# Five pairs of 16-bit products of 512 columns taken out of the second attention

## The chip, the cores and the metric

The kernel runs on one core of a Trainium2 chip. The metric is the device time of one execution in microseconds (us). Three executions of the kernel before took 310.08, 311.3 and 319.42 us, median 311.3. TensorE is written PE below, VectorE DVE, ScalarE ACT, GpSimd POOL.

## The reference

The input x has four sequences (b = 0 to 3) of 256 tokens with 256 channels, in 32-bit floats. Four layers follow each other, and each of them starts with the same gating step:

```
x = x + attn0(cond(x))        # 16 heads of 16 columns, softmax over rows and over columns
x = x + ffn0(cond2(x))        # 8-bit product of 256 by 256, and a bias
x = x + attn1(cond(x))        # rotary, block mask, softmax, 16 heads
x = x + ffn1(cond2(x))        # BitLinear: h = relu(xq w1)^2 (1024 wide), then hq w2
```

cond is a running weighted sum over time, forward and backward, that is divided and multiplied by a sigmoid of x. In ffn1 the weights are rounded to -1, 0 and 1 and the activations are scaled by the largest value of each row, so each row has to be known before it can be quantised.

The kernel writes only the final x. The products that the change takes out have a result that nothing reads: they belong to no term of the reference.

## The kernel before, in words

Each engine has a program of its own, and the programs meet by semaphores. The order of the work is written out by hand, in slots. In the second attention and the last layer a slot is one value of `p` in `for p in SLOTS1`, from -8 to 41; the programs of PE, ACT, DVE and POOL all run over the same `p`. Slots 0 to 31 are the 32 pairs of heads (8 for each sequence). Tables such as `HID_AT`, `TURN_AT`, `DOWN_AT`, `X_AT` say in which slot a piece of the last layer for tile t (128 rows) or sequence b is done, so the last layer of a sequence runs beside the attention of the next ones.

PE does, in this order in each slot: the scores of the slot (`scores1`, L1436), the turning of an attention output (`turn_y1`, L1475), the approximate scores from which a row maximum is taken for a slot four later (`maxima`, L1415), the transposes of queries (`turn_again`, L1467), probabilities by values (`values1`, L1451), the turning of finished rows (`turn_rows`, L1208), projections of the next sequence, then the pair of products of the change, and last the last layer: `turn_hidden` (L1538), `turn_x` (L1514), `hidden` (L1529), `down` (L1552). The scores wait for ACT's exponential of the slot before (L661); `maxima` waits for DVE's row maximum (L981) and for DVE's `relu` (L1034) where both use the same bank; `hidden` waits for DVE's row maxima; `turn_x` waits for DVE's quantised rows (L1015); `down` waits for copies by ACT (L589) or DVE (L1020), and its result is added by DVE at L1063.

The helper `whole(bank, n)` issues n products of a 128x128 16-bit identity with 512 columns of a 16-bit weight tile, into a bank of PSUM; nobody reads the result. It is called in several places: before and in the first feed-forward layer, in slots -4 to -1, twice in each of the slots 23 to 27, and three times in each of the slots 36, 38, 40 and 41. In slots 23 to 27 it stands behind a wait for `g3_done` at 2, which ACT reaches in slot 20, and it writes bank 0 of `PM`, which no other instruction uses in those slots.

POOL starts the DMAs that add the backward to the forward sums, and SP those that load and store; neither runs in step with these products.

Of the kernel before, what the change touches and what calls it, by code (L numbers as in the profile page):

```python
# [71 lines left out]
def build(nc, xT_d, kT_d, vec_d, cond_d, gains_d, gcol_d, attn0_d, attn0p_d, ffn0_d, bias0_d, attn1_d, w1_d, w2_d,  # L72
          ident_d, rope_d, out_d):
    ctx = ExitStack()
    with ctx:
# [3 lines left out]
        S = {n: ctx.enter_context(nc.semaphore(n)) for n in LOADS + STEPS}  # L79
# [107 lines left out]
        PM = ctx.enter_context(nc.psum_tensor("PM", [P, 2, 512], F32))  # L187
# [68 lines left out]
        def tiles(table, p):  # L256
            return [t for t, at in enumerate(table) if at == p]

        def again_at(p):
            q, odd = divmod(p + 2, 2)  # L260
            return [] if odd or not 0 <= q < B * CH else [divmod(q, CH)]

        def turny_at(p):
            return tiles(TURNY_AT, p)
# [856 lines left out]
        def _(pe):  # L1121
# [83 lines left out]
            def turn_rows(q, bank, ready, done):  # L1205
                pe.wait_ge(S[ready], q + 1)
                for u in range(TT):
                    ins = nc.tensor.transpose(PO[:, bank, T + u * P:T + (u + 1) * P], yc[:, q % 2, u * P:(u + 1) * P],  # L1208
                                              ident[:])
                ins.then_inc(S[done], 1)  # L1210
# [111 lines left out]
            def whole(bank, n):  # L1322
                for i in range(n):
                    nc.tensor.matmul(bank, identb[:], w1q[:, 0:512], start=True, stop=True)
# [66 lines left out]
            def maxima(n):  # L1391

                b, j = divmod(n, PAIRS)
                c = j // 2
                if j == 0:
                    pe.wait_ge(S["kTb_done"], b + 1)
                    pe.wait_ge(S["qTb_done"], b + 1)
                if n == 0:
                    pe.wait_ge(S["y8_done"], B)
                    pe.wait_ge(S["v1_done"], 1)  # L1400
                elif n == 1:
                    pe.wait_ge(S["kT1_done"], 1)
                elif n == 2:
                    pe.wait_ge(S["negmax_done"], 2)
                else:
                    pe.wait_ge(S["negmax_done"], 2 * n)
                rounded = [t for t, at in enumerate(HID_AT) if at < n - LEAD]
                if rounded:
                    pe.wait_ge(S["relu_done"], len(rounded))
                at0 = max_bank(n)  # L1410
                q, k = qTb[b % 2], kTb[b % 2]
                for u in range(TT):
                    for i in range(2):
                        r = SLOT * (2 * (j % 2) + i)
                        ins = nc.tensor.matmul(PS[:, at0 + i, u * P:(2 * u + 1) * P],  # L1415
                                               q[r:r + ROWS, c, u * P:(u + 1) * P],
                                               k[r:r + ROWS, c, 0:(u + 1) * P], start=True, stop=True)
                ins.then_inc(S["mx_mm_done"], 1)

            def scores1(p):  # L1420

                b, j = divmod(p, PAIRS)
                c = j // 2
                if j % 2 == 0:
                    pe.wait_ge(S["po1_free"], PO1["again", b, c] + 1)
                if j == 0:
                    pe.wait_ge(S["kT1_done"], b + 1)
                if p == 0:
                    pe.wait_ge(S["negmax_done"], 4)
                q, k = qT1[b % 2], kT1[b % 3]  # L1430
                for v in range(TT):
                    for i in range(2):
                        if v == 0 and p >= 1:
                            pe.wait_ge(S["e1_done"], 2 * (p - 1) + i + 1)
                        r = SLOT * (2 * (j % 2) + i)
                        ins = nc.tensor.matmul(PS[:, i, 2 * v * P:2 * P + v * P], k[r:r + ROWS, c, v * P:(v + 1) * P],  # L1436
                                               q[r:r + ROWS, c, v * P:2 * P], start=True, stop=True)
                        if v == TT - 1:
                            ins.then_inc(S["s1_done"], 1)

            def values1(q):
                b, c = divmod(q, CH)
                pe.wait_ge(S["e1_done"], 4 * q + 4)
                if c == 0:
                    pe.wait_ge(S["v1_done"], b + 1)
                    pe.wait_ge(S["v_ones"], 1)
                if q >= 1:
                    pe.wait_ge(S["y1_done"], q)
                for v, q0, col in ((0, 0, 0), (1, P, 2 * P)):
                    for g in range(4):  # L1450
                        ins = nc.tensor.matmul(PO[SLOT * g:SLOT * (g + 1), 0, q0:T], vt[:, b % 3, v * H + 4 * c + g, :],  # L1451
                                               E[:, (2 * q + g // 2) % 4, g % 2, col:col + T - q0],
                                               start=(v == 0), stop=(v == TT - 1))
                ins.then_inc(S["pv1_done"], 1)
# [7 lines left out]
            def turn_again(b, c):  # L1462
                pe.wait_ge(S["negmax_done"], 2 * (PAIRS * b + 2 * c + 2))
                free1(("again", b, c), downs(PAIRS * b + 2 * c - 2))
                for u in range(TT):
                    src = kp[:, b % 2, u * H + 4 * c:u * H + 4 * c + 4, :]
                    ins = nc.tensor.transpose(PO[:, 1, u * P:(u + 1) * P], src.rearrange("p g s -> p (g s)"), ident[:])  # L1467
                ins.then_inc(S["qre_done"], 1)

            def turn_y1(b):  # L1470
                pe.wait_ge(S["y1_done"], CH * (b + 1))
                free1(("rows", b), downs(TURNY_AT[b]))
                for h in range(HALF):
                    for u in range(TT):
                        ins = nc.tensor.transpose(PO[:, 1, h * T + u * P:h * T + (u + 1) * P],  # L1475
                                                  ytok[:, u, h * P:(h + 1) * P], ident[:])
                ins.then_inc(S["ytr1_done"], 1)
# [78 lines left out]
            for p in SLOTS1:  # L1556
                b, j = p // PAIRS, p % PAIRS
                if -LEAD <= p < 0:
                    whole(PO[:, 0], 3)
                if 0 <= p < B * PAIRS:  # L1560
                    scores1(p)
                for bb in turny_at(p):
                    turn_y1(bb)
                if 0 <= p + LEAD < B * PAIRS:
                    maxima(p + LEAD)
                for bb, c in again_at(p):
                    turn_again(bb, c)
                if p % 2 == 0 and 0 <= (p - 2) // 2 < B * CH:
                    values1((p - 2) // 2)
                if p % 2 == 1 and 0 <= (p - 3) // 2 < B * CH:  # L1570
                    turn_rows((p - 3) // 2, 0, "rows1_done", "turned1_done")
                for t in tiles(QK_AT, p):
                    project_qk(t // TT, t % TT)
                if j == 1 and b + 1 < B:
                    project_v(b + 1)
                if p == -PAIRS + 2:
                    turn_both()
                if j == 2 and 0 < b + 1 < B:
                    turn(b + 1, 0, "qtr_done", [("qkp_done", 2 * TT * (b + 2)), ("v1_done", b + 2),
                                                ("rope_done", TT * (b + 2)), ("v_ones", 1)])  # L1580
                if j == 3 and 0 < b + 1 < B:
                    turn(b + 1, TT * H, "ktr_done", [("qTb_done", b + 2)])
                for bb in tiles(G3_AT, p):
                    turn_gates(bb)
                for bb in tiles(STATE_AT, p):
                    state_rows(bb)
                for bb in tiles(PROJ_AT, p):
                    project_rows(bb)
                if p in (23, 24, 25, 26, 27):
                    pe.wait_ge(S["g3_done"], 2)  # L1590
                    whole(PM[:, 0], 2)
                if p in (36, 38, 40, 41):
                    pe.wait_ge(S["g3_done"], B)
                    whole(PM[:, 0], 3)
                for t in tiles(TURN_AT, p):
                    turn_hidden(t)
                for bb in tiles(X_AT, p):
                    turn_x(bb)
                for t in tiles(HID_AT, p):
                    hidden(t)  # L1600
                for t in tiles(DOWN_AT, p):
                    down(t)
# [59 lines left out]
```

## Time and profile before

| | |
|---|---|
| median of three executions | 311.3 us (310.08 to 319.42) |
| profiled execution, its own time | 313.35 us |
| its span, from first to last instruction | 311.5 us |
| PE busy | 266.2 us (85%) |
| DVE busy | 254.0 us (82%) |
| ACT busy | 204.7 us (66%) |
| POOL busy | 37.1 us (12%) |
| mean granted TensorE clock | 0.949 of full speed |
| chain that ended last | PE 46%, DVE 27%, ACT 13%, issue 9%, DMA 3% |

The profiled execution is one execution: 1.85 us of its time lie outside the span. Busy PE counts a product from its issue to the modelled end of its pipeline, so a product of 0.38 us may block its follower for less. The granted clock is 1.00 at 2.4 GHz and 0.50 at 1.2 GHz. In the profiled execution it was at 0.50 from 34.1 to 37.5 us, 68.2 to 71.6, 109.2 to 112.6, 177.5 to 184.3, 221.8 to 225.2, and from 300.3 us to the end; elsewhere after the start it was at 1.00. Slots 23 to 27 take the time from 246.5 to 265.4 us.

### The profile page before, as it was taken

How to read it: one execution, taken by the hardware profiler on the slowest of the kernel's cores; microseconds unless marked ns; L12 is line 12 of the kernel's file. 1: busy time of each engine (PE TensorE's matmuls, PEld its weight loads, DVE VectorE, ACT ScalarE, POOL GpSimd, SP SyncE). 2: the span in 40 equal slices, each digit the busy share in tenths (PEclk: the TensorE clock that was granted, in tenths of full speed). 3: DMA queues.
4: the chain of work that ended last, by engine and by line, in shares of the span. 5: the costliest groups of instructions: out<-in, count | busy, mean ns of one | idle time of the engine just before them, and what ended most of it. 6: DMA issues, size and time to landing. Idle time of an engine off the chain costs nothing.

```text
span 311.5 us, 6280 instructions
## 1 busy us (share of the span) xinstructions
PE 266.2 (85%) x2425; PEld 159.6 (51%) x2425; DVE 254.0 (82%) x492; ACT 204.7 (66%) x354; POOL 37.1 (12%) x63
## 2 busy tenths in 40 slices
PE   7989786769999899797999898899799878988655
PEld 2344453445566455453556545675566644756422
DVE  1999799958999979868999979979978786567761
ACT  3786768898898877915557563885366756753331
POOL 1300112111212121030010114201400100000000
PEclk9999799989999979999999869999799999999975
DMA  4940244633495573030020625333300440000000
GB/s 130 386 175 2 47 92 89 115 69 69 93 245 104 105 135 69 2 67 0 0 54 17 121 50 102 69 69 67 67 2 1 86 84 3 2 17 19 18 17 34
DMA packets 8237, 22.55 MB, mean 72 GB/s; under 512 B 1552, under 2 KB 2960, under 8 KB 7824
## 3 DMA queue, kind: packets, MB, share of 16 engines
q0 software_dynamic: 4032, 14.68, 25.2%
q1 hardware_dynamic: 4176, 7.48, 6.6%
q8 instruction: 19, 0.31, 0.4%
q14 instruction: 10, 0.08, 0.1%
HBM read 6.43 MB, written 1.05 MB: 24 GB/s over the span
## 4 chain that ended last, share of the span: by engine, by line
PE 46%; DVE 27%; ACT 13%; issue 9%; DMA 3%; SPq 1%; DVEq 0%; ACTq 0%; POOLq 0%
PE PM L1239 5%; PE PM L1353 4%; PE PS L1436 4%; DVE kp L981 4%; PE PO L1186 3%; PE PO L1199 3%; PE PS L1171 3%; PE PO L1451 2%; PE PM L1131 2%; DVE bwd L751 2%; DVE fwd L741 2%; PE PO L1208 2%; PE PS L1529 2%; ACT E L536 2%; DMA xT<-in_xT 2%
## 5 line engine op out<-in xcount | busy, mean ns | idle before, releaser
L536 ACT ACTIVATE E<-PS,negc,escale 128x1024 f32<-128x1024 f32 x32 | 38.3, 1200 | 11.1 <-PE PS L1171 11.0
L661 ACT ACTIVATE E<-PS 128x384 f32<-128x384 f32 x64 | 27.8, 488 | 16.4 <-PE PS L1436 16.4
L981 DVE TENSOR_REDUCE kp<-PS 128x2 f32<-128x256 f32 x64 | 32.4, 548 | 5.5 <-PE PS L1415 5.3
L333 POOL DMA_DIRECT2D fwd<-mid x14 | 12.2, 872 | 107.2 <-DVE fwd L741 107.2
L339 POOL DMA_DIRECT2D fwd<-bwd x14 | 12.5, 891 | 84.0 <-DVE bwd L751 45.9
L1186 PE MATMUL PO<-E,kp 128*32 128x256 f32 x256 | 18.1, 401 | 2.7 <-ACT E L536 2.4
L741 DVE TENSOR_TENSOR_SCAN fwd<-DT,ekv 128x512 f32<-128x512 f32 x16 | 19.8, 1240 | 0.0
L741 DVE TENSOR_TENSOR_SCAN fwd<-DT,ek 128x512 f32<-128x512 f32 x16 | 19.7, 1229 | 0.0
L1171 PE MATMUL PS<-TP 32*128 32x256 f16 x256 | 19.4, 274 | 0.0
L751 DVE TENSOR_TENSOR_SCAN bwd<-ekv,DT 128x511 f32<-128x511 f32 x16 | 19.3, 1206 | 0.0
L751 DVE TENSOR_TENSOR_SCAN bwd<-ek,DT 128x511 f32<-128x511 f32 x16 | 19.2, 1203 | 0.0
L1353 PE MATMUL PM<-G,sg 128*128 128x512 f32 x32 | 17.1, 666 | 2.0 <-DVE sg L759 2.0
L1208 PE MATMUL PO<-ident,yc 128*128 128x128 f32 x64 | 14.0, 301 | 4.9 <-ACT yc L513 4.9
L1199 PE MATMUL PO<-E,vr 128*32 128x256 f32 x256 | 17.2, 386 | 0.9 <-ACT yB L519 0.9
L1415 PE MATMUL PS<-E 32*128 32x256 bf16 (+1 forms) x128 | 10.9, 247 | 6.8 <-DVE kp L981 4.1
L1436 PE MATMUL PS<-w,TP 32*128 32x128 f32 (+1 forms) x128 | 15.4, 347 | 1.4 <-ACT E L661 1.4
L1552 PE MATMUL PO<-wq,kT 128*128 128x256 bf16 x64 | 10.0, 308 | 7.2 <-ACT kT L589 5.0
L1171 PEld LDWEIGHTS PS<-TP 32*128 32x128 f16 x256 | 9.9, 93 | 12.1 <-issue 9.8
L1436 PE MATMUL PS<-TP 32*128 32x256 f32 (+1 forms) x128 | 15.4, 348 | 0.6 <-ACT E L661 0.6
L1436 PEld LDWEIGHTS PS<-w,TP 32*128 32x128 f32 x128 | 11.5, 184 | 7.5 <-issue 4.7
L1436 PEld LDWEIGHTS PS<-TP 32*128 32x128 f32 x128 | 11.8, 185 | 7.0 <-issue 5.9
L513 ACT ACTIVATE yc<-PO 128x256 f32<-128x256 f32 x32 | 12.5, 391 | 2.9 <-PE PO L1186 1.9
(220 smaller groups left out, 607.7 us busy)
## 6 DMA issues: line engine op xcount, KB each, us to landing
fwd<-mid POOLq DMA_DIRECT2D x14, 512.0 KB, 4.6
fwd<-bwd POOLq DMA_DIRECT2D x14, 512.0 KB, 4.5
kT<-in_kT SPq DMA_DIRECT2D x4, 256.0 KB, 6.7
xT<-in_xT SPq DMA_DIRECT2D x4, 256.0 KB, 5.2
G<-in_w SPq DMA_DIRECT2D x1, 1024.0 KB, 9.4
vt<-in_w SPq DMA_DIRECT2D x1, 1024.0 KB, 11.2
G<-in_attn SPq DMA_DIRECT2D x1, 1024.0 KB, 7.7
out<-ek SPq DMA_DIRECT2D x8, 128.0 KB, 1.7
```

What stands on the lines that cost most here:

```text
L536: nc.scalar.activation(E[:, p % 6], PS[:, 2 * (p % 2):2 * (p % 2) + 2, :], ACT.Exp, bias=negc[:], scale=escale[:]).then_inc(S["e0_done"], 1)
L661: nc.scalar.activation(E[:, p % 4, i, 0:384], PS[:, i, 0:384], ACT.Exp, scale=QSCALE).then_inc(S["e1_done"], 1)
L741: nc.vector.tensor_tensor_scan(fwd[:, r, i], DT[n % 2][:, 0:SEG], src[:, seg(b)], 0.0, ALU.mult, ALU.add).then_inc(S["scan_done"], 1)
L751: nc.vector.tensor_tensor_scan(bwd[:, n % 2, i, 0:SEG - 1][:, ::-1], src[:, seg(b, 1, SEG - 1)][:, ::-1], DT[n % 2][:, 1:SEG][:, ::-1], 0. ...
L981: nc.vector.tensor_reduce(kp[:, b % 2, u * H + 2 * j:u * H + 2 * j + 2, D], PS[:, at0:at0 + 2, lo:hi], AX, ALU.max, negate=True).then_inc( ...
L1171: ins = nc.tensor.matmul(PS[:, 2 * (p % 2) + i, u * T:(u + 1) * T], khl[b % 2][r:r + SLOT, c, u * P:(u + 1) * P], q[b % 2][r:r + SLOT, c, ...
L1186: ins = nc.tensor.matmul(PO[SLOT * g:SLOT * (g + 1), 0, 0:T], kv[:, b % 2, v * H + 4 * c + g, D:WIDE], E[:, (2 * q + g // 2) % 6, g % 2, v ...
L1199: ins = nc.tensor.matmul(PO[SLOT * g:SLOT * (g + 1), 1, at:at + T], vr[:, q % 2, v * 4 + g, :], E[:, (2 * q + g // 2) % 6, g % 2, v * T:(v ...
L1208: ins = nc.tensor.transpose(PO[:, bank, T + u * P:T + (u + 1) * P], yc[:, q % 2, u * P:(u + 1) * P], ident[:])
L1239: ins = nc.tensor.matmul(PM[:, 1, o * T:(o + 1) * T], w[:, k, o * P:(o + 1) * P], src[:, k, :], start=(part == 0 and k == 0 and o == 0), s ...
L1353: ins = nc.tensor.matmul(PM[:, u, :], sg[:, seg(b, k * T + u * P, P)], w1a[:, k, 0:2, :].rearrange("p n c -> p (n c)"), start=(k == 0), st ...
L1436: ins = nc.tensor.matmul(PS[:, i, 2 * v * P:2 * P + v * P], k[r:r + ROWS, c, v * P:(v + 1) * P], q[r:r + ROWS, c, v * P:2 * P], start=True ...
```

## The change

Three lines of PE's program are taken out: the condition, the wait and the call. That is ten products and their ten weight loads. The calls of `whole` in all other places stay, and no other engine's program is changed.

```diff
                 for bb in tiles(PROJ_AT, p):
                     project_rows(bb)
-                if p in (23, 24, 25, 26, 27):
-                    pe.wait_ge(S["g3_done"], 2)
-                    whole(PM[:, 0], 2)
                 if p in (36, 38, 40, 41):
                     pe.wait_ge(S["g3_done"], B)
                     whole(PM[:, 0], 3)
```

## Rows read from the trace of the kernel before

**Rows 1.** The page's granted TensorE clock in 40 slices, in tenths.

```profile
PEclk9999799989999979999999869999799999999975
```

**Rows 2.** Timeline of PE in slots 23 to 27: start, us, operation, [idle before, releaser].

```profile
247.77 0.59 PE L1324 MATMUL PM<-wq,identb 128*128 128x512 bf16 x2
...
251.10 0.60 PE L1324 MATMUL PM<-wq,identb 128*128 128x512 bf16 x2
252.28 0.38 PE L1514 MATMUL PO<-identb,vr 128*128 128x128 bf16 x4 [0.57 <-DVE vr L1015]
...
254.38 0.92 PE L1436 MATMUL PS<-w,TP 32*128 32x256 f32 x8
...
255.67 0.59 PE L1324 MATMUL PM<-wq,identb 128*128 128x512 bf16 x2
256.82 1.02 PE L1529 MATMUL PS<-wq,yB 128*128 128x512 bf16 x4 [0.56 <-DVE kp L981]
...
260.69 0.60 PE L1324 MATMUL PM<-wq,identb 128*128 128x512 bf16 x2
...
263.21 0.59 PE L1324 MATMUL PM<-wq,identb 128*128 128x512 bf16 x2
264.41 1.02 PE L1529 MATMUL PS<-wq,yB 128*128 128x512 bf16 x4 [0.60 <-DVE kp L981]
```

**Rows 3.** Chain of waits in order of time, 247 to 266 us: start, us, what.

```profile
252.05 0.93 DVE kp L981 x2
...
253.41 1.05 PE PO L1552 x8
...
255.63 0.94 DVE kp L981 x2
...
256.82 1.04 PE PS L1529 x4
...
259.26 0.34 PE PS L1415 x4
...
260.76 0.54 PE PM L1324 x2
...
263.05 1.03 DVE kp L981 x2
...
264.41 1.02 PE PS L1529 x4
```

**Rows 4.** PE in chosen stretches: stretch, length, busy (count), clock, DMA share, GB/s.

```profile
174.40:177.40 3.00, 2.47 (x22) 1.00 0.15 30
218.80:221.80 3.00, 1.32 (x15) 1.00 0.00 0
...
142.00:145.00 3.00, 1.01 (x4) 1.00 0.00 0
250.00:253.00 3.00, 2.09 (x24) 1.00 0.93 175
...
256.00:259.00 3.00, 2.14 (x14) 1.00 0.13 43
```

**Rows 5.** PE in half microseconds about one fall of the clock.

```profile
221.50:222.00 0.50, 0.50 (x7) 0.83 0.00 0
...
225.00:225.50 0.50, 0.50 (x3) 0.76 0.03 0
```

**Rows 6.** Chain of waits over the whole span: the same product, full and half clock.

```profile
163.63 1.74 PE PM L1366 x8
...
222.13 3.33 PE PM L1366 x8
```

**Rows 7.** The same chain, a product of the last layer at half clock.

```profile
301.75 1.89 PE PO L1552 x8
```

**Rows 8.** Timeline of all engines, 240 to 270 us, ACT and DVE.

```profile
248.85 1.02 ACT L589 ACTIVATE kT<-PO 128x1024 bf16<-128x1024 bf16 x1 [0.49 <-PE PO L1538]
...
260.11 0.85 ACT L661 ACTIVATE E<-PS 128x384 f32<-128x384 f32 x2
...
263.05 1.02 DVE L981 TENSOR_REDUCE kp<-PS 128x2 f32<-128x256 f32 x2 [1.33 <-PE PS L1415]
```

**Rows 9.** Timeline of PE, 172 to 186 us, about the longest fall but the last.

```profile
177.92 0.50 PE L1415 MATMUL PS<-E 32*128 32x128 bf16 x4 [0.98 <-DVE kp L981]
```

## The prediction

> **What bounds the kernel now.** I began with the engines' busy times: PE is busy for 85% of the span and DVE for 82%, and the chain that ended last runs over PE for 46% and over DVE for 27%. So neither is the bound alone; work is handed to and fro, and ten products on PE can lie on the path or beside it. Next I read the granted clock over the whole span [rows 1]: it is mostly full, with dips at a few places, and low at the end. So the removed products have two possible uses of time: what PE spends on them, and what they do for the clock. The third view is PE's own timeline over slots 23 to 27 [rows 2]: the ten products stand there as five pairs, and the reader is to look at the instruction behind each, whether it starts at once or after an idle stretch that another engine ends. The fourth is the chain in order of time [rows 3]: which of the five pairs has a piece of its own in it. Last come PE's busy time in short stretches [rows 4, 5] and pairs of equal work at both clocks [rows 6, 7].
>
> **The pairs, one by one.** Each takes 0.59 or 0.60 us in the timeline, overlapping its follower a little [rows 2]; the one that the chain shows takes 0.54 us there [rows 3]. All five together would be 5 x 0.54 = 2.7 us, the most that the removal can give if all lay on the path.
>
> Slot 23 (247.77): behind it comes the turning of hidden rows, which ACT copies at 248.85 after an idle 0.49 us that PE ended [rows 8]. This copy would come up to 0.54 us earlier and so would PE's next turning and values, but then PE stands for 0.57 us for DVE's quantised rows (L1015) [rows 2]. DVE doesn't wait there: the chain of this time runs through its row maxima at 252.05 [rows 3]. Gain 0; if DVE's cover were gone, 0.54.
>
> Slot 24 (251.10): the same wait of 0.57 us stands right behind it. PE would only wait longer. Gain 0. Slot 25 (255.67): PE then stands for 0.56 us until the row maxima, which started at 255.63, are done [rows 2, 3]. Gain 0. Slot 27 (263.21): PE stands for 0.60 us behind it, again for DVE's row maxima [rows 2]. Gain 0.
>
> Slot 26 (260.69) is the one on the chain. From 259.26 to 263.05 us the chain is PE without a gap, seven pieces, and this pair is the 0.54 us among them [rows 3]. DVE at 263.05 had been idle for 1.33 us and can start earlier [rows 8], and the wait of 0.60 us in slot 27 moves with it. But the scores that follow need both halves of ACT's exponential, which ends at 260.11 + 0.85 = 260.96 us [rows 8]. If all of the scores had to wait for that, they would start at about 261.03 instead of 261.30 (where the chain's piece ends): 0.27 us. Only the second head needs the later half and the first head's product can fill the time, so the gain lies between 0.27 and 0.54; I take **0.45 us**, nearer to the upper end because the first head's first product fits in before. The removed wait for `g3_done` was met slots earlier and costs nothing either way. No DMA is issued or moved.
>
> **The clock.** Without the pairs the stretch is thinner. From 250 to 253 us PE was busy 2.09 us of 3, of which 0.60 us are the pair of slot 24: 1.49 us are left. From 256 to 259 it was 2.14, of which some 0.27 us are the tail of the pair of slot 25 (255.67 + 0.59 = 256.26): 1.88 left [rows 2, 4]. The clock did fall right after 174.4 to 177.4 us, with 2.47 us busy, and after 218.8 to 221.8 us, with 1.32. It held after 142 to 145 us with 1.01 us, but those were full products with little else about them [rows 4]. So busy time alone doesn't decide; what went before the two falls was mostly small products (scores and maxima on 32 rows, values on 32 columns) and waits for DVE's row maxima [rows 9], and this is what slots 23 to 27 consist of once the full 128-row, 512-column pairs are gone. The pairs are the densest work PE has there apart from the last layer's. I expect the clock to fall at least once between 250 and 267 us in most executions.
>
> What a fall costs is in the rows. The one at 221.8 us lasts from about 221.7 to 225.2 [rows 5], and one projection on the chain took 3.33 us in it, against 1.74 us at full clock [rows 6]: 1.59 us. A product of the last layer took 1.89 us instead of 1.05 [rows 3, 7]: 0.84. A fall in slots 23 to 24, where DVE is the chain, could cost 0; one in which PE is the chain throughout 1.6. After 252 us the stretch is mostly PE or PE and DVE in turns, so I take 1.6 for one fall, and 0 and 1.6 as its bounds. **Sum:** -0.45 + 1.6 = +1.15 us. Against the profiled execution of 313.35 us that is 314.5. That execution lies 2.05 us above the median of the three shown, which spread by more than this from each other; put against the median, 311.3 + 1.15 = **312.5 us**.
>
> At the page "TensorE: Matmul & The Clock Gate" (section "Why this matters for your kernels") the Trainium skill speaks against this: it ties drops in mid-kernel to long idle gaps of PE between bursts, and the gaps here would stay short. By that rule the sum is the 0.45 us alone, 310.9 us. At the fall of 177.5 us PE's idle time was 0.98 us, up to 177.92 [rows 9], after 2.47 us busy in 3 [rows 4], so this trace doesn't bear the rule out as the only cause.
>
> **Rivals.**
>
> No fall. The other waits keep PE busy enough, the pairs were ballast, and only slot 26 gives: 311.3 - 0.45 = 310.9 us. For it: 142 to 145 us [rows 4], and thin stretches that held. Against it: 174.4 to 177.4, busier than what is left here.
>
> Two falls, one about slots 24 and 25 and one about 26 and 27, with recovery between: 311.3 - 0.45 + 2 x 1.6 = 314.1 us. For it: both places lose a pair, and the pairs stand 3 to 5 us apart [rows 2], so that no one place is left as it was.
>
> The clock falls at slot 24 and stays down until the dense projections after 267 us: slower by over 2%. Precedents are the 6.8 us from 177.5 to 184.3 and the end of the kernel, where it doesn't come back [rows 1]. The price is the PE pieces of the chain once more: L1552 1.05, L1529 1.04, the seven pieces 3.79 less the pair's 0.54, L1529 again 1.02 [rows 3], together 6.36 us; and the scores and maxima from 254.38 us on, which now end just before DVE needs them at 255.63 and would, at twice 0.92 us and with the maxima behind them, be about 1.1 us late [rows 2, 3]. That is 311.3 - 0.45 + 7.5 = 318.3 us. It decides only if the clock is low by about 254 us and does not recover in the full products of slot 25.
>
> The end gets better. The last fall at 300.3 us goes away, because everything after slot 26 stands 0.45 us earlier. One product of the last layer loses 0.84 us there [rows 7]; with the second one alike and about 1.1 us for the turning and the last extra products between them, 2.8 us: 311.3 - 0.45 - 2.8 = 308.0 us. Against it: the waits there for ACT and DVE are long, and nothing in them changes.
>
> **How the numbers follow.** One fall 0.42, no fall 0.24, two falls 0.20, clock stays down 0.08, a better end 0.06. The predicted time is that of one fall, 312.5 us. The range takes in no fall (310.9) and two falls (314.1), each with the scatter of executions of 1 to 2 us that the profiled one and the lower two of the median show (310.08 to 313.35), and part of the way to 318.3: 309.3 to 316.8 us. Left out are the better end and the low clock throughout, and some scatter beyond. Two per cent, about what a measurement of this kernel can tell from no change, is 6.2 us. Slower by over 2% (above 317.5) needs the clock to stay down: 0.08. Faster by over 2% (below 305.1) is reached by no case, only by scatter on the better end: 0.02. Within 2%: 0.90.
>
> **What would show it.** In the changed kernel's trace the chain should have no piece for L1324 between 246 and 266 us, the idle times before L1514, L1529 and L1529 [rows 2] should grow to about 1.0 to 1.15 us, and the scores of slot 27 should start at about 260.8 with their later part waiting for L661. The clock of 5 us stretches between 250 and 270 us should be below 1.00 at least once. If it stays at 1.00 there in several executions and the time still rises, the mechanism is wrong; if the clock falls and the time doesn't rise, DVE covers more than I say; if it falls where all fillers stand too, their place was never the cause. The prediction is wrong in its size if one fall brings the next with it.

## The result and the profile after

The changed kernel took 323.01 us in the median of six executions (317.89 to 323.47), the kernel before 311.77 us (six, 310.08 to 319.42). The ratio is 1.027, with a 95% interval of 1.020 to 1.035. The ratio of the two medians is larger, 1.036, because the ratio with the interval leaves out executions more than 1.5% above the fastest of their kernel, and the fastest here, 317.89, stands well below the other five. The forecast was 312.5 us, in a range of 309.3 to 316.8.

The profiled execution after took 322.77 us with a span of 321.0. This is its granted clock in 40 slices, to be read against [rows 1]:

```profile
PEclk9999998979999799999999599799799955599995
```

Slices 33 to 35 (of 8 us each) are new: three slices at about half clock in a row. In microseconds, PE alone (stretch, length, busy and count, clock, DMA share, GB/s):

```profile
250.00:255.00 5.00, 3.58 (x46) 1.00 0.59 124
255.00:260.00 5.00, 4.13 (x22) 0.55 0.13 37
260.00:265.00 5.00, 3.92 (x19) 0.50 0.00 0
265.00:270.00 5.00, 5.00 (x35) 0.50 0.01 2
270.00:275.00 5.00, 3.92 (x15) 0.50 0.00 0
275.00:280.00 5.00, 5.00 (x34) 0.56 0.01 3
280.00:285.00 5.00, 5.00 (x50) 1.00 0.00 0
```

The clock fell at 255.5 us and came back at 279.4: 23.9 us at 1.2 GHz, where the kernel before had none at all between 225.2 and 300.3 us. The timeline of PE shows what runs there, and answers to [rows 2]. A count of x3 at L1529, where four products are issued, means that the record of one is missing. The scores behind it come 1.42 us after its start here and 1.80 us where all four are recorded at this clock, so it is the first that is missing: the start reads some 0.4 us late, and the idle time before it is 0.70 us and not 1.08.

```profile
254.56 0.40 PE L1514 MATMUL PO<-identb,vr 128*128 128x128 bf16 x4 [1.38 <-DVE vr L1015]
255.87 1.86 PE L1552 MATMUL PO<-wq,kT 128*128 128x256 bf16 x8 [0.91 <-DVE yB L1020]
257.66 1.65 PE L1436 MATMUL PS<-w,TP 32*128 32x256 f32 x8
...
261.33 1.49 PE L1529 MATMUL PS<-wq,yB 128*128 128x512 bf16 x3 [1.08 <-DVE kp L981]
...
276.61 1.12 PE L1487 MATMUL PM<-ident,G 128*128 128x128 f32 x4
277.52 1.92 PE L1497 MATMUL PM<-ident,xT 128*128 128x128 f32 x8
279.23 1.96 PE L1504 MATMUL PM<-G,yT 128*128 128x256 f32 x8
281.12 0.92 PE L1436 MATMUL PS<-w,TP 32*128 32x256 f32 x8
```

The place of the pair of slot 24 is now an idle stretch of 1.38 us before L1514 and 0.91 before L1552, against 0.57 before L1514 in [rows 2] and 0.75 before L1552 in this line of the kernel before:

```profile
253.41 1.03 PE L1552 MATMUL PO<-wq,kT 128*128 128x256 bf16 x8 [0.75 <-DVE yB L1020]
```

Right behind it the groups of products take 1.6 to 1.8 times as long, L1552 1.86 us against 1.03 and the scores 1.65 against 0.92. The clock came back under the turning and projection of slot 28 (L1487, L1497, L1504), the first long run of 128-row, 128-column products in the stretch. Idle time alone did not keep it down: from 265 to 270 us PE is busy without a gap, and the clock stayed at 0.50. The chain of the stretch (start, us, what), against [rows 3]:

```profile
254.50 0.93 DVE kp L981 x2
...
255.87 1.86 PE PO L1552 x8
257.73 1.58 PE PS L1436 x8
...
259.67 1.04 DVE kp L981 x2
...
261.33 1.49 PE PS L1529 x3
262.82 1.58 PE PS L1436 x8
...
265.36 1.44 PE PO L1451 x16
266.80 1.58 PE PS L1436 x8
...
271.56 1.48 PE PS L1529 x3
```

The scores at 257.73 us (L1436, 1.58 us) are on the chain, where before DVE's work alone was: they stood beside it at full clock. The span grew by 9.5 us, and the two timelines of PE place them. A slot is taken to begin with its scores. Slot 23 begins 2.44 us later (248.92 against 246.48); that part lies ahead of the removed products, where the two programs are the same, so it is scatter: one fall at 47.3 and one at 200.9 us that the execution before hadn't, one at 34.1 that it had and this one hadn't. Slot 28 begins 7.60 us later, slot 29 10.54: slots 23 to 27 cost 5.16 us and slot 28 another 2.94, together 8.1. Over the rest 1.04 us are won back, since the last fall comes later in the work: L1552 at 312.29 still takes 1.05 us where it took 1.89 [rows 7].

```profile
312.29 1.05 PE PO L1552 x8
```

### The profile page after: what moved, and what is told of

It is laid out like the page before. It is cut to its first block, busy times and chain, and to the rows that moved or that the text cites. A ratio compares the mean times of both kernels' runs of the same rounds, so it can differ in the third digit from the quotient of the medians.

```text
span 321.0 us, 6247 instructions
## 1 busy us (share of the span) xinstructions
PE 271.3 (85%) x2402; PEld 163.3 (51%) x2415; DVE 254.1 (79%) x492; ACT 205.0 (64%) x354; POOL 37.1 (12%) x63
## 3 DMA queue, kind: packets, MB, share of 16 engines
HBM read 6.43 MB, written 1.05 MB: 23 GB/s over the span
## 4 chain that ended last, share of the span: by engine, by line
PE 46%; DVE 26%; ACT 12%; issue 10%; DMA 4%; SPq 1%; DVEq 0%; ACTq 0%; POOLq 0%
PE PS L1436 5%; PE PM L1239 5%; PE PM L1353 4%; DVE kp L981 4%; PE PO L1186 3%; PE PO L1451 3%; PE PO L1199 3%; PE PS L1171 3%; PE PS L1529 2%; DVE bwd L751 2%; DVE fwd L741 2%; PE PO L1208 2%; ACT E L536 2%; DMA xT<-in_xT 2%; PE PM L1131 2%
## 5 line engine op out<-in xcount | busy, mean ns | idle before, releaser
L981 DVE TENSOR_REDUCE kp<-PS 128x2 f32<-128x256 f32 x64 | 32.4, 548 | 11.2 <-PE PS L1415 11.0
L1186 PE MATMUL PO<-E,kp 128*32 128x256 f32 x256 | 18.9, 417 | 2.7 <-ACT E L536 2.3
L1436 PE MATMUL PS<-w,TP 32*128 32x128 f32 (+1 forms) x128 | 18.6, 404 | 2.5 <-ACT E L661 2.5
L1436 PEld LDWEIGHTS PS<-w,TP 32*128 32x128 f32 x128 | 13.9, 221 | 10.2 <-issue 5.9
L1208 PE MATMUL PO<-ident,yc 128*128 128x128 f32 x64 | 14.7, 314 | 4.9 <-ACT yc L513 4.9
L1353 PE MATMUL PM<-G,sg 128*128 128x512 f32 x32 | 17.1, 666 | 2.0 <-DVE sg L759 2.0
L1415 PE MATMUL PS<-E 32*128 32x256 bf16 (+1 forms) x128 | 11.6, 260 | 6.1 <-DVE kp L981 4.1
L1552 PE MATMUL PO<-wq,kT 128*128 128x256 bf16 x64 | 10.0, 308 | 7.3 <-ACT kT L589 5.0
L1436 PE MATMUL PS<-TP 32*128 32x256 f32 (+1 forms) x128 | 15.4, 348 | 0.6 <-ACT E L661 0.6
L1451 PE MATMUL PO<-E,vt 128*32 128x256 f32 (+1 forms) x256 | 15.7, 369 | 0.0
```

The costliest lines, as they stand in the source:

```text
L981: nc.vector.tensor_reduce(kp[:, b % 2, u * H + 2 * j:u * H + 2 * j + 2, D], PS[:, at0:at0 + 2, lo:hi], AX, ALU.max, negate=True).then_inc( ...
L1186: ins = nc.tensor.matmul(PO[SLOT * g:SLOT * (g + 1), 0, 0:T], kv[:, b % 2, v * H + 4 * c + g, D:WIDE], E[:, (2 * q + g // 2) % 6, g % 2, v ...
L1353: ins = nc.tensor.matmul(PM[:, u, :], sg[:, seg(b, k * T + u * P, P)], w1a[:, k, 0:2, :].rearrange("p n c -> p (n c)"), start=(k == 0), st ...
```

## The experiments

All kernels here differ from the kernel before (B) by the edit shown. Nothing reads the products in question, so none leaves out part of the reference. The median of B in the same sets of executions lay between 313.1 and 314.2 us, higher than at first; the ratios are each against B on the same chip.

The times of whole executions mix the stretch in question with falls of the clock elsewhere. In the profiles of the kernels that are the same up to slot 23, that slot begins anywhere from 243.03 us (four) to 248.92 (the changed kernel). So the table gives, from each kernel's one profiled execution, the time on PE's timeline from the scores of slot 23 to those of slot 29, and how long the clock was at 0.50 in it. Each is one execution.

| kernel | pairs in slots 23 to 27 | slot 23 to 29, us | at half clock in it, us |
|---|---|---|---|
| B | all five | 24.10 | 0 |
| keep24_25 | 24, 25 | 23.82 | 0 |
| four | all five, four products each | 24.70 | 0 |
| keep24 | 24 | 29.01 | 13.7 |
| keep25 | 25 | 29.15 | 6.8 and 6.8 |
| burst26 | none, ten products in 26 | 30.29 | 13.7 |
| narrow | all five, 32 rows by 32 columns | 31.26 | 17.1 |
| changed kernel | none | 32.20 | 23.9 |
| keep26_27 | 26, 27 | 32.48 | 23.9 |
| more | all five | 24.04 | 0 |
| more_no_pairs | none | 32.23 | 23.9 |

**Pairs in slots 24 and 25 alone** (keep24_25)

```diff
-                if p in (23, 24, 25, 26, 27):
+                if p in (24, 25):
```

> The pairs stand only in slots 24 and 25 (four products, not ten). Theory A: the clock falls in the thin stretch of slots 24 and 25, and once low it stays low because the hand-offs between PE and DVE leave PE too thin to bring it back before the projections of slot 28. Then these two pairs prevent the fall there; slots 26 and 27 are left bare, so a fall may come there in about a third of the executions and would last some 10 us: median 311 to 314 us, some executions up to 318. Theory B: what counts is the total of PE work in the slots; with 4 of 10 products left the loss is about 6 of 10 of the measured 11 us: 317 to 319 us in all executions. Theory C: most of the difference came from dips elsewhere by the accident of when they fell: no relation to the pairs, 312 to 323 us.

Measured: 313.34 us (ten executions, 311.16 to 314.39), B 314.17, ratio 0.9997 (0.994 to 1.006). No fall between 224 and 298 us in its profile. The pairs of slots 23, 26 and 27 can go without loss, so theory B (total of work) is out. It also shows what the pairs of slots 26 and 27 had cost, since the clock is full on both sides:

```profile
257.81 0.34 PE L1415 MATMUL PS<-E 32*128 32x128 bf16 x4 [0.56 <-DVE fwd L1034]
...
262.88 0.81 PE L1529 MATMUL PS<-wq,yB 128*128 128x512 bf16 x3 [1.17 <-ACT yT L615]
263.62 0.92 PE L1436 MATMUL PS<-w,TP 32*128 32x256 f32 x8
```

L1529 again lacks its first record, so the scores of slot 28 behind it are the mark to measure to. In B they stand here:

```profile
265.37 0.92 PE L1436 MATMUL PS<-w,TP 32*128 32x256 f32 x8
```

From L1415 of slot 26 to these scores it is 263.62 - 257.81 = 5.81 us, against 265.37 - 259.26 = 6.11 in B [rows 2, 3]: the gain is 0.30 us. Over slots 23 to 28 it is 0.28 us (23.82 against 24.10), so the pair of slot 23 gave nothing. The chain of this stretch runs through ACT, from one exponential to the next:

```profile
258.66 0.85 ACT E L661 x2
259.51 0.27 ACT w L622
259.79 0.27 ACT yc L513
260.06 0.62 ACT fwd L439
...
261.24 0.85 ACT E L661 x2
262.09 0.50 ACT yT L615
```

ACT starts that second exponential 3.43 us after L1415 in both kernels (in B at 262.69 us). DVE's row maximum of slot 27 (L981) starts 3.57 us after L1415 instead of 3.79. DVE could come earlier and ACT did not, and now ACT's copy (L615) is the last that L1529 waits for.

**Pairs in slots 26 and 27 alone** (keep26_27)

```diff
-                if p in (23, 24, 25, 26, 27):
+                if p in (26, 27):
```

> The pairs stand only in slots 26 and 27. Theory A: the fall at slots 24 and 25 still comes (granted clock 0.50 from about 253 to 257 us), but the pairs in 26 and 27 bring the clock back sooner than in the changed kernel, where it stayed down for 23.9 us: 5 to 15 us low, 315 to 320 us. If two pairs are too little to bring it back once PE runs at half clock, it is the time of the changed kernel, 321 to 323. Theory B (total of work): 317 to 319 us, as with the pairs in 24 and 25.

Measured: 317.54 us (316.35 to 318.93), ratio 1.015 (1.004 to 1.026). The clock fell at 250.7 us and was low for 23.9 us, as long as in the changed kernel (5 to 15 us were expected): two pairs after the fall didn't bring it back.

```profile
250.00:255.00 5.00, 3.86 (x24) 0.57 0.23 46
255.00:260.00 5.00, 3.92 (x21) 0.50 0.05 18
260.00:265.00 5.00, 5.00 (x35) 0.50 0.00 2
265.00:270.00 5.00, 4.78 (x19) 0.50 0.00 0
```

The time is in the range that theories A and B share, so it alone decided nothing; the clock did. The same number of products in slots 24 and 25 cost nothing, so their place counts and not their number. Theory A had tied a clock as low as this to 321 to 323 us. From slot 23 to slot 29 the kernel did take as long as the changed one (32.48 us against 32.20); the changed kernel's profiled execution began slot 23 4.33 us later, in a part that is the same in both. The pair of slot 27 and L1529 behind it, from 267.3 to 269.7 us, did not bring the clock back; it came back at 274.6 us, again under slot 28's turning and projection.

**The same products on a sixteenth of the array** (narrow)

```diff
+            def narrow(n):
+                for i in range(n):
+                    nc.tensor.matmul(PM[0:SLOT, 0], identb[0:SLOT, 0:SLOT], w1q[0:SLOT, 0:512], start=True, stop=True)
...
-                    whole(PM[:, 0], 2)
+                    narrow(2)
```

> All ten products stand in their places with 512 columns each, but take 32 rows by 32 columns of the array (one sixteenth of its cells); PE's time and order are those of the kernel before. Theory A in its sharper form: what keeps the clock up is how much of the array works, so the clock falls as in the changed kernel and the time is 320 to 324 us. Rival D: what keeps it up is that PE is occupied at all (or the pacing, the 0.54 us by which the following work is held back): clock as in the kernel before, 310 to 313 us.

Measured: 319.31 us (318.52 to 320.14), ratio 1.022 (1.010 to 1.034); none of its four executions is as fast as the slowest of B's 19 executions in this set (316.62). PE's order and durations are those of B up to the fall, and its waits are no longer by more than 0.02 us:

```profile
249.34 0.60 PE L1324 MATMUL PM<-wq,identb 32*32 32x512 bf16 x2
250.52 0.38 PE L1518 MATMUL PO<-identb,vr 128*128 128x128 bf16 x4 [0.58 <-DVE vr L1015]
...
253.81 0.60 PE L1324 MATMUL PM<-wq,identb 32*32 32x512 bf16 x2
255.09 0.81 PE L1533 MATMUL PS<-wq,yB 128*128 128x512 bf16 x3 [0.68 <-DVE kp L981]
255.83 0.92 PE L1440 MATMUL PS<-w,TP 32*128 32x256 f32 x8
257.31 0.44 PE L1419 MATMUL PS<-E 32*128 32x128 bf16 x4 [0.57 <-DVE fwd L1034]
```

(L1518 and L1533 are B's L1514 and L1529. L1533 lacks its first record, so its 0.68 us are some 0.46.) The first pair shown takes 0.60 us and the wait behind it is 0.58 us, as in [rows 2], yet the clock fell at 257.4 us and was low for 17.1 us. Rival D, that PE need only be occupied, or that the pairs pace the hand-offs, is out. What makes the difference is in the shape: these products use a sixteenth of the array. Rows, columns and the weight loads (32 columns instead of 128) were cut together, so which of them counts isn't shown. The narrow products aren't quite as good as none either: the fall came after slot 25's L1529, as with the pair of slot 24 alone, and not in slot 24 as with no pairs, and the time is just under the 320 to 324 us that theory A gave.

**Four products instead of two** (four)

```diff
-                    whole(PM[:, 0], 2)
+                    whole(PM[:, 0], 4)
```

> Four products instead of two in each of slots 23 to 27. Theory A: no fall in slots 23 to 27 already with two, so nothing is won for the clock; the ten further products cost 0.43 us each slot where PE is the chain (slot 26) and are beside DVE in the others up to the idle 0.57 us: 311.5 to 313.5 us. Theory B (total of work raises the clock elsewhere): 309 to 311 us.

Measured: 312.82 us (ten executions, 309.08 to 320.65), ratio 0.994 (0.988 to 1.001): no difference that this can tell. Its executions spread widely: five of the ten took 309.1 to 311.6 us, the others 314.0 to 320.7. In its profile there is no fall in slots 23 to 27, and slots 23 to 28 take 24.70 us against B's 24.10: the ten more products cost 0.6 us there and win nothing sure elsewhere.

**One pair, in slot 24 or in slot 25** (keep24, keep25)

```diff
-                if p in (23, 24, 25, 26, 27):
+                if p in (24,):        # the other kernel: (25,)
```

> One pair, in slot 24 alone. With the pairs of slots 24 and 25 the time was that of the kernel before (ratio 0.9997). Theory A (the fall begins where PE waits for DVE's quantised rows in slot 24): this one pair is enough, 311 to 315 us. Rival E (both places count, since the stretch between 250 and 260 us has to be thick throughout): the clock falls a little later, from about 257 us, and stays down for 15 to 20 us: 316 to 321 us.

> One pair, in slot 25 alone. Theory A: the fall about 251 to 255 us comes and lasts to the projections of slot 28, 318 to 323 us. Rival E: either place alone gives some of it, and the time is that of the pair in slot 24 alone.

Measured: slot 24 alone 317.13 us (315.77 to 318.16), ratio 1.011 (1.006 to 1.017); slot 25 alone 316.94 us (313.11 to 320.63), too spread for an interval. With slot 24's pair the clock fell at 258.4 us, not about 251, and was low for 13.7 us (15 to 20 were expected). With slot 25's it fell at 251.7, was back at 258.5 and fell again at 265.3 until 272.2. Rival E holds: both places count, and theory A's claim that the wait in slot 24 is enough was wrong. In the kernel with slot 25's pair the clock came back while that pair and L1529 ran one behind the other; the half and full durations meet within L1529. That these six products brought it back isn't shown, for the same two groups in slot 27 of keep26_27 did not:

```profile
256.53 1.06 PE L1324 MATMUL PM<-wq,identb 128*128 128x512 bf16 x2
257.44 1.54 PE L1529 MATMUL PS<-wq,yB 128*128 128x512 bf16 x4
258.91 0.92 PE L1436 MATMUL PS<-w,TP 32*128 32x256 f32 x8
```

**A burst after the fall** (burst26)

```diff
-                if p in (23, 24, 25, 26, 27):
+                if p in (26,):
...
-                    whole(PM[:, 0], 2)
+                    whole(PM[:, 0], 10)
```

> No pairs, but ten full products together in slot 26. The clock falls at about 251 to 255 us as in the changed kernel. Theory A (it stays down because the handed-over work is too thin to bring it back): the ten products, 4.3 us at half clock, bring it back at slot 26 or 27, so it is low for 10 to 17 us and not 23.9, at the price of the burst on the chain: 316 to 320 us. Rival F (the clock comes back after a length of its own, whatever runs): low for 20 to 24 us and the burst comes on top: 323 to 327 us.

Measured: 316.78 us (316.46 and 317.11), ratio 1.010 (1.003 to 1.018). The clock fell at 250.9 us, as in keep26_27, and came back at 264.6, within the burst:

```profile
261.22 1.51 PE L1451 MATMUL PO<-E,vt 128*32 128x256 f32 x16
262.66 3.27 PE L1324 MATMUL PM<-wq,identb 128*128 128x512 bf16 x10
265.86 0.92 PE L1436 MATMUL PS<-w,TP 32*128 32x256 f32 x8
```

L1451 is still at half clock (1.51 us), the scores behind the burst at full (0.92). The clock was low for 13.7 us instead of 23.9: in keep26_27, where it fell at the same time (250.7 us), it came back 10 us later. Slots 23 to 28 take 30.29 us, 1.9 less than in the changed kernel, though 3.3 us of useless work stand on the chain; the median is some 6 us lower, but in the two profiled executions 4.07 us of that stand ahead of slot 23, where the programs are the same. Rival F, a length of its own, is out. In the six profiles in which the clock fell in these slots and no burst was added (the changed kernel, keep26_27, keep24, keep25, narrow, more_no_pairs) the last fall of the stretch ended under slot 28's turning and projection. So in all seven a run of full products ended it. How long a run it takes isn't shown: the 2.4 us of slot 27 in keep26_27 were not enough.

**Full products ahead of the other falls of B** (more)

```diff
+                if p == 6:
+                    pe.wait_ge(S["kT1_done"], 2)
+                    whole(PM[:, 0], 4)
+                if p == 17:
+                    pe.wait_ge(S["rope_done"], 7)
+                    whole(PM[:, 0], 5)
                 if 0 <= p + LEAD < B * PAIRS:
                     maxima(p + LEAD)
...
+                if p == 5:
+                    pe.wait_ge(S["kT1_done"], 2)
+                    whole(PM[:, 0], 2)
                 if p in (23, 24, 25, 26, 27):
...
-                    whole(PM[:, 0], 3)
+                    whole(PM[:, 0], 7 if p == 40 else 3)
...
+                if p in (40, 41):
+                    whole(PM[:, 0], 8 if p == 40 else 4)
                 for t in tiles(DOWN_AT, p):
                     down(t)
```

> The kernel before with full products added where PE stands idle ahead of its other falls: 2 at the end of slot 5, 4 before the maxima of slot 6, 5 before the maxima of slot 17, 7 instead of 3 in slot 40, and 8 and 4 between the turning and the last product of slots 40 and 41. Theory A: the falls at about 177, 221 and 300 us go, which cost about 2.7, 1.6 and 2.8 us in the kernel before; the additions lie in idle time of PE save some tenths: 304 to 309 us. Rival: falls come elsewhere instead, or the additions delay the chain: 311 to 315 us.

Measured: 307.19 us (306.76 to 311.21), B 313.94, ratio 0.983 (0.975 to 0.990). The profiled execution took 306.88 us; its clock and the stretch where B's last fall was:

```profile
PEclk9999997999999999999999998999999999999999
```

```profile
294.89 0.62 PE L1538 MATMUL PO<-identb,kT 128*128 128x128 bf16 x8 [0.48 <-DVE kT L1052]
295.35 1.89 PE L1324 MATMUL PM<-wq,identb 128*128 128x512 bf16 x8
298.03 1.05 PE L1552 MATMUL PO<-wq,kT 128*128 128x256 bf16 x8 [0.79 <-ACT kT L589]
```

The falls at 177 and 221 us are gone, one at 188.4 us is new, and the last one is put off to 304.4 us, behind PE's last product; the last two L1552 take 1.05 us each instead of 1.89 [rows 7]. The two profiled spans differ by 6.4 us (305.1 against 311.5), but only half of that stands behind the edit: slot 5, where the first product is added, begins 3.23 us earlier (170.81 against 174.04), in a part that is the same in both. Of the other 3.2 us, 2.7 are won from the last `turn_hidden` but one to the end (10.21 us against 12.89), and only 0.5 in all that lies between. So what these two executions show is that the end gets better; that the products of slots 5, 6 and 17 pay isn't shown.

**Three products more, in slot 9** (more9)

Against the kernel with more products:

```diff
+                if p == 9:
+                    pe.wait_ge(S["rope_done"], 5)
+                    whole(PM[:, 0], 3)
```

> The kernel with more products (307.19 us, ratio 0.9826) and three further ones before the maxima of slot 9, where PE stands idle for 0.8 us and where the clock fell at 188 to 191 us in three of the kernels. Theory A: one fall less where it comes, 1 to 2 us: 305 to 307.5 us. Rival: the scatter of the executions hides it or another dip takes its place, 307 to 308.5 us.

Measured: 309.3 us (ten executions, 306.87 to 311.97), B 313.09, ratio 0.992 (0.987 to 0.997). A miss: no better than the kernel with more products. Its profiled execution has no fall at 188 us, but was low from 195.8 to 206.0 us, some 10 us behind the place that was filled. Whether the three products brought this about isn't shown. Both kernels are faster than B, this one by 0.8% (0.3 to 1.3), the one without the three products by 1.7% (1.0 to 2.5).

**The five pairs out of the kernel with more products** (more_no_pairs)

Against the kernel with more products:

```diff
-                if p in (23, 24, 25, 26, 27):
+                if p in ():
```

> The kernel with more products, but without the five pairs of slots 23 to 27. Theory A (the long stretch at half clock is the work of those slots alone and has nothing to do with the dips before it): the clock is at full until about 245 us, falls between 246 and 256 us and stays down for 14 to 24 us; 8 to 11 us are lost against 307.2: 315 to 318 us. Rival C (the removal's price came in good part from dips in other slots, which the added products now prevent): 309 to 312 us.

Measured: 315.15 us (314.82 to 315.36), ratio 1.013 (1.001 to 1.025). The median is 8.0 us above that of the kernel with more products, which was measured on another chip; the two ratios, 1.013 and 0.983, put some 9.5 us between them. Its clock:

```profile
PEclk9999997999999999999999997999999955599999
```

It fell at 249.2 us and was low for 23.9 us. Slots 23 to 28 take 32.23 us against 24.04 with the pairs, 8.2 us more, where the two first timelines gave 8.1. Both profiles have the same two falls ahead of it, at 48 and 188 us. Rival C is out as the main cause: the removal costs 8 us by itself. The rest of the 11.2 us between the first two medians isn't placed; 2.44 us of it stood ahead of slot 23 in the profiled execution.

## Why the prediction was wrong, step by step

**The two uses of the pairs** were seen, and the sign of the sum was right. The first sign of it, a fall between 250 and 267 us, came in both profiles without the pairs (255.5 us, and 249.2 in the last kernel, which runs some 6 us ahead there), and the chain has no piece for L1324 left. The idle times before L1514 and L1529 were to grow to 1.0 to 1.15 us. Before L1514 it was 1.38, because the pair of slot 23 shows there too (with that pair gone and slot 24's in place, in keep24_25, it was 0.84); before L1529 it was 0.99 where the clock was still full (keep24), and 0.70 at half clock.

**The step that failed** is the one fall at 1.6 us as the likeliest case. It took its length and its price from the fall at 221.8 us [rows 5, 6], which ended after 3.4 us; the measured one lasted 23.9 us and cost 8.1. At 221.8 us a long projection of full products follows (L1366); in slots 24 to 27 none does. The rival in which the clock stays down had the right mechanism, and was given 0.08. What spoke for it stood in the same rows: the fall at 177.5 us lasted 6.8 us, and nothing in the stretch after 253 us looked like L1366, only single groups of some 1 us (L1552, L1529). burst26 shows that the missing dense work is what kept the clock down: with ten full products it came back 10 us earlier. What makes it fall at just that place is shown only as far as that two full pairs, in slots 24 and 25, prevent it and one of them does not.

**The price** of that rival, 7.5 less 0.45, that is 7.0 us, looks close to the measured 8.1 by luck: two misses stand against each other. For slots 23 to 27 it was too high, 7.0 against 5.16 us. It doubled every piece of PE on the chain, while they took 1.7 to 1.9 times as long (L1467 0.62 us against 0.37, L1451 1.44 against 0.79), and PE's waits in between took up part of it: the 0.57 us before L1415 at 259.26 us in B are gone at half clock. For slot 28 it had nothing, though it let the clock stay down to the projections there; the scores, the turning, the values and the projection itself cost 2.94 us more.

**The 0.45 us** for slot 26 measured 0.30 (keep24_25). That lies between its bounds of 0.27 and 0.54, but for another reason than the one given. The working asked of ACT only when its exponential of slot 26 ends. It left out that ACT goes on without a pause with two copies and the logarithm and exponential of the gate (L439, L442) before the exponential of slot 27 and the copy L615, for which L1529 then waits. In B the two ran level, ACT's copy ending at 264.04 us and DVE's row maxima at 264.07, so the chain named only one of them.

**Slots 23, 24, 25 and 27 at 0.** For slots 23 and 27 this was right for the pairs' own time: keep24_25 (no 23, 26, 27) is at 0.9997, and its gain is the one above. For slots 24 and 25 no run shows it, since without either pair the clock falls.

**The rule of the Trainium skill** (page "TensorE: Matmul & The Clock Gate", section "Why this matters for your kernels"), which ties a drop to long idle gaps, gave 310.9 us. It isn't what happened. In narrow the idle times of PE in slots 24 and 25 were at most 0.58 and 0.68 us, about those of B, and the clock fell. The prediction was right not to build its sum on it; the brief fall came from the rows, not from this rule.

**Chances.** Slower by over 2% got 0.08 because it hung on a single case; with the length of a fall taken from what follows it, that case should have been the likeliest. How far beyond the range the median came, 323.0 against 316.8 us, is in part scatter: keep26_27 has the same long fall and a ratio of 1.015, the changed kernel 1.027.

## What to carry to other kernels

When work that holds the clock is taken out, look for where the clock would come back, not only for where it falls. In this kernel that was the next long run of full-array products, 24 us on, and the cost was what PE had on the chain up to there, each piece some 1.7 to 1.9 times as long, less what other engines' work still covered. Products that nobody reads are worth trying in PE's idle time right before such a stretch: two of them in each of two slots were enough here, in one slot they were not, and ten of 32 rows by 32 columns didn't do. Compare executions by the stretch that the edit touches; the rest of the program moved by up to 5.9 us between profiles of the same code. A piece on the chain of waits is worth its length only if no other engine runs level with it.

## What the runs showed of the hardware that was not expected

Equal durations of PE weren't equal for the clock: with ten products of 32 rows by 32 columns in the same places, at the same 0.60 us a pair, it was low for 17.1 us, with ten of 128 by 128 not at all. At half clock the chain of small products with waits for DVE, though PE counts as busy 3.9 to 5.0 us of 5, didn't bring the clock back in 23.9 us. Executions of one kernel differ by a few per cent: B ranged from 309.99 to 316.62 us in one set, with a mean granted clock between 0.969 and 0.939. Only one of B's executions was profiled, but the profiles of other kernels, which are the same as B up to slot 23, have their early falls at other times or fewer of them.
